# Two attentions of a one-core kernel: 64x64 tiles in the first, denominators inverted in compact form in the second

## The chip, the core and the metric

The kernel runs on one NeuronCore of a Trainium2 chip. The core has a matrix engine (TensorE, PE in the profile), a vector engine (VectorE, DVE), a scalar engine (ScalarE, ACT), a general engine (GpSimd, POOL) and a queue that only issues transfers (SyncE, SP). TensorE writes its results to PSUM, eight banks of 512 float32 a partition, which VectorE and ScalarE read. The metric is the device time of one execution, in microseconds (us). Lower is better.

## What is computed

Four layers run one after the other on 2 x 1024 tokens of 128 features, each with a normalisation before it and a residual around it: an attention of 16 heads of 64 features, a feed-forward layer with weights quantised to four bits, mixture-of-experts layers of 16 experts, and between them a second attention of 16 heads of 8 features with a bias by distance. The change touches the two attentions. The first one:

```python
def _L0_attn_ref(x, Wq, Wk, Wv, Wo):
    H, DH = (16, 64); SOFTCLAMP = 50.0; SCALE = DH ** (-0.5)
    q = jnp.einsum('bnd,fd->bnf', x, Wq).reshape(b, n, H, DH).transpose(0, 2, 1, 3)
    ...  # k and v alike, from Wk and Wv
    sim = jnp.einsum('bhid,bhjd->bhij', q, k) * SCALE
    sim = SOFTCLAMP * jnp.tanh(sim / SOFTCLAMP)
    sim = jnp.where(jnp.tril(jnp.ones((n, n), dtype=bool)), sim, jnp.finfo(sim.dtype).min)
    out = jnp.einsum('bhij,bhjd->bhid', jax.nn.softmax(sim, axis=-1), v)
    return jnp.einsum('bnf,df->bnd', out.transpose(0, 2, 1, 3).reshape(b, n, H * DH), Wo)
```

And the core of the second:

```python
    bias = slopes[:, None, None] * jnp.minimum(idx[None, :] - idx[:, None], 0)
    scores = jnp.einsum('bhtd,bhsd->bhts', q, k) / math.sqrt(D) + bias[None]
    y = jnp.einsum('bhts,bhsd->bhtd', jax.nn.softmax(scores, axis=-1), v)
    return y.transpose(0, 2, 1, 3).reshape(B, T, C) @ W_proj + b_proj
```

Both softmaxes are divided out at the end: the exponentials are multiplied with the values, and the product is scaled by the inverse of their sum.

## The kernel before

Everything is written out by hand: each engine has its own program, the engines wait for each other on counters (semaphores), and an engine does its work in the order in which it is written.

**First attention** (`stage_front`). Heads are taken in pairs, two heads side by side in 128 partitions, and each pair has two batches: 16 passes `s = 2 * p + b`, in `pair(p, more)`. The first and the last pair are written out, the six between them are a loop (`Fori`), in which waits go against a register. The lower triangle of 8 x 8 blocks of 128 x 128 is cut into NU = 9 units a pass (`PIECES`), each 512 columns wide. For a unit TensorE makes the scores of both heads (`scores`, L774: 64 rows of the array by 128 columns for each head, written 64\*128), ScalarE does tanh and exp (L486, L491), POOL masks the diagonal (L463), VectorE and POOL add up the exponentials (L403, one head each), and TensorE multiplies with the values (`multiply`, L786: 128 rows by 64 columns a head, 128\*64). `project` makes queries, keys and values of the next pass (L756, L762, also 128\*64), `totals` the sums over keys (L798, 128\*32), `out` the final product (L836). The order on TensorE goes by slots of two units: scores of the next two units, a piece of `project`, products of these two. `take` (L496, ScalarE) copies the product out of its two banks, which there are once. A float32 matmul is two instructions on the chip, so four matmuls are eight records in a profile.

**Second attention** (`stage_alibi_attention`). 16 halves `hs` of eight units `gu`, four heads together. TensorE makes scores twice: once 12 units ahead for the maxima (`max_pair`, L2112), which VectorE reduces (`reduce_chunk`, L1977, four a unit) out of a ring of three banks, and once for the exponentials (L2136, L2140); ScalarE does exp (L1911), and TensorE multiplies with values and a row of ones (L2157), so that the denominators come out beside the product. The SP queue lays each half's maxima into rows (`maxima_rows`, L1671), loads the rows of the scores of coming steps (L1686, L1727), and in `keep_out` stores a finished half to memory and loads it again in another arrangement (L1753, L1756), the denominators of four heads spread over eight features each (L1757). In `divide(k)`, for k in order 3, 0, 1, 2, VectorE inverts a quarter of them as 128 x 512 (L1994) and multiplies (L1996); three quarters after unit 117, the last after unit 124. `project_out(k)` (L2190) waits for them, on TensorE after units 119 and 126. The last half goes through `select_last` (L2167) and `divide_last` (L2002, L2005).

Of the kernel before, what the change touches and what calls it, by code (L numbers as in the profile page):

```python
# [42 lines left out]
def bcast(ap, shape):  # L43
    return ap.broadcast_to(shape)
# [133 lines left out]
class QuantFfn:  # L178
# [89 lines left out]
    def next_keep(self, act, k):  # L268
# [11 lines left out]
PIECES = [[(0, 0, 0, 512)], [(0, 0, 512, 512)],  # L280
# [4 lines left out]
NU = len(PIECES)  # L285

DIAGS = [[at for J, at, q, w in u if q == P * J] for u in PIECES]
ADDS = [[(0, 128, (0, 0), None)],
        [],
        [(512, 512, (1, 0), (2, 0))],  # L290
        [(128, 384, (0, 128), (3, 0)), (896, 128, None, (3, 384))],
        [(512, 512, None, (4, 0))],
        [(256, 256, None, (5, 0)), (768, 256, None, (5, 256))],
        [(512, 512, None, (6, 0))],
        [(384, 128, None, (7, 0)), (640, 384, None, (7, 128))],
        [(512, 512, None, (8, 0))]]
# [3 lines left out]
SLOTS = NU  # L300

# [7 lines left out]
def stage_front(nc, g, sem):  # L309
# [11 lines left out]
     z.multiplied, z.taken, z.summedA, z.summedB, z.totalled, z.copied, z.spread, z.inverted, z.kept,  # L321
     z.broad, z.scaled, z.wo, z.summed, z.added) = (
        sem("at0_" + x) for x in (
        "w ones pooled projected query key value scored clamped exped masked multiplied taken summedA summedB "
        "totalled copied spread inverted kept broad scaled wo summed added").split())
    with ExitStack() as tmp:
# [56 lines left out]

        def add_up(eng, s, b, u, h, done):
# [5 lines left out]
            for k, (to, w, first, second) in enumerate(ADDS[u]):  # L390
                into = ACC[b][:, h, to:to + w]
                if second is None:
                    if h == 1:

                        eng.sem_inc(z.pooled, 1)
                    eng.tensor_copy(into, PR[first[0]][:, h, first[1]:first[1] + w]).then_inc(done, 1)
                    continue
# [3 lines left out]
                else:  # L401
                    old = PR[first[0]][:, h, first[1]:first[1] + w]
                eng.tensor_tensor(into, old, PR[second[0]][:, h, second[1]:second[1] + w], ALU.add).then_inc(done, 1)  # L403

        with nc.Block() as block:
# [48 lines left out]
            def _(pool):  # L454
                def mask(s, u):
# [4 lines left out]
                    even = DIAGS[u] == [0, 2 * P]  # L460
                    for at in DIAGS[u][0:1] if even else DIAGS[u]:
                        blocks = v[:, at // P::2 if even else 4, :]
                        last = pool.affine_select(out=blocks, in_=blocks, compare_op=ALU.is_ge, fill=0.0, base=0,  # L463
                                                  pattern=[[0, 4 if even else 2], [1, P]], channel_multiplier=-1)
# [14 lines left out]
            def _(act):  # L479
                def clamp(s, b, u):  # L480
                    act.wait_ge(z.scored, NU * s + u + 1)
                    wait(act, z.multiplied, NU * (s - 1) + u + 1)
                    through = ADDED[max(u, 3) + 1] - ADDED[NU]
# [9 lines left out]
                def take(s, b, p, half):  # L493

                    act.wait_ge(z.multiplied, NU * s + NU - 1 + half)
# [3 lines left out]
                def pair(p, more):  # L499
                    for k in range(SLOTS):  # L500
# [4 lines left out]
                        if k == 0 and not (isinstance(p, int) and p == 0):  # L505
                            for half in range(2):
                                take(2 * p - 1, 1, p - 1, half)
                        if k in (4, 5):
                            take(2 * p, 0, p, k - 4)
# [103 lines left out]
            def _(dve):  # L613
# [11 lines left out]

                def copy_totals(s):
# [14 lines left out]
                def pair(p, more):  # L641
                    first = isinstance(p, int) and p == 0
                    for k in range(SLOTS):
                        for s, b, u in slot(p, k):
                            add_up(dve, s, b, u, 0, z.summedA)
                        if k < 3 or 4 <= k < 7 and more:
                            projected(2 * p + 1 + k // 4, 1 - k // 4, 2 * (k % 4))
                            projected(2 * p + 1 + k // 4, 1 - k // 4, 2 * (k % 4) + 1)
                        if not first:
                            if k == 0:  # L650
                                invert(2 * p - 2)
# [1761 lines left out]
```

## Time and profile before

| | us |
|---|---|
| median of 3 runs | 1230.98 |
| lowest and highest run | 1230.45, 1236.72 |
| the profiled execution, its own time | 1236.2 |
| its span, first to last instruction | 1234.5 |

A row of a timeline has the start in us, the length in us, the engine, the line of the kernel, the instruction, what it writes and reads, shape and count; idle time before it and who ended it stand in brackets. PEld are the loads of weights into the array, which run beside matmuls. A row of several instructions covers them from the first start to the last end. In the profiled execution the first attention's passes run from about 58 to 431 us, the second attention's stage from about 642 to 1070 us.

### The profile page before, as it was taken

The numbers are of one execution on the slowest core, as the hardware profiler recorded it, in microseconds if no ns is written. First come the engines' busy times: TensorE is split into PE (matmuls) and PEld (weight loads), VectorE is DVE, ScalarE is ACT, GpSimd is POOL, SyncE is SP. The second block draws the span as 40 slices with busy tenths as digits, with TensorE's granted clock in tenths as the row PEclk, the third lists the DMA queues.
The fourth block names the chain that finished last, engine by engine and source line by source line (L and its number), as shares of the span: only waits on it lengthen the run. The fifth ranks groups of instructions, "written<-read, shape, count | busy, mean of one in ns | idle before, by whom it ended". The sixth has DMA issues, their size and how long they took to land. (4 is left out here: it accounts for less than half of the span.)

```text
span 1234.5 us, 21616 instructions
## 1 busy us (share of the span) xinstructions
PE 1149.7 (93%) x7431; PEld 576.2 (47%) x7431; DVE 850.4 (69%) x1779; ACT 718.9 (58%) x944; POOL 531.2 (43%) x577
## 2 busy tenths in 40 slices
PE   4899999999999998879997999999999998787998
PEld 1444444444444485368984222222222222546896
DVE  6366667666666555864426899999999996585442
ACT  3687787787787615612215177777777776451221
POOL 0056656656756700338853014322422331035884
PEclk9899999999999998979999999999999998697999
DMA  4001001001011100427752212211121110223765
GB/s 127 1 7 25 19 24 41 18 24 38 21 24 35 30 25 6 170 65 194 178 116 63 71 42 61 65 53 54 56 60 58 55 38 14 92 84 99 194 171 122
DMA packets 56194, 81.41 MB, mean 66 GB/s; under 512 B 19348, under 2 KB 37144, under 8 KB 55472
## 3 DMA queue, kind: packets, MB, share of 16 engines
q1 hardware_dynamic: 44040, 70.30, 18.6%
q0 software_dynamic: 10880, 8.86, 4.9%
q10 hardware_dynamic: 1192, 1.19, 0.3%
q8 instruction: 48, 0.79, 0.3%
q14 instruction: 34, 0.28, 0.1%
HBM read 55.02 MB, written 15.60 MB: 57 GB/s over the span
## 5 line engine op out<-in xcount | busy, mean ns | idle before, releaser
L1911 ACT ACTIVATE at_PR<-psum 128x1024 f32<-128x1024 f32 x256 | 248.1, 1021 | 110.8 <-PE psum L2140 108.8
L1977 DVE TENSOR_REDUCE at_MX<-psum 128x1 f32<-128x512 f32 x468 | 298.7, 685 | 11.3 <-PE psum L2112 8.1
L486 ACT ACTIVATE PR<-psum 128x1024 f32<-128x1024 f32 x144 | 141.0, 1027 | 73.5 <-PE psum L774 60.2
L774 PE MATMUL psum<-Q,K 64*128 64x512 f32 (+3 forms) x768 | 143.5, 502 | 1.2 <-ACT PR L486 1.2
L491 ACT ACTIVATE PR<-PR 128x1024 f32<-128x1024 f32 x144 | 144.6, 1062 | 0.0
L786 PE MATMUL psum<-PR,V 128*64 128x512 f32 (+3 forms) x768 | 137.4, 489 | 0.1
L2157 PE MATMUL psum<-at_PR,at_VG 128*32 128x512 f32 x1024 | 136.8, 607 | 0.0
L1848 POOL TENSOR_TENSOR at_PR<-at_PR,at_FAC 128x512 f32<-128x512 f32 x64 | 81.2, 1268 | 107.1 <-ACT at_PR L1911 107.1
L463 POOL TENSOR_SCALAR_AFFINE_SELECT PR<-PR 128x256 f32<-128x256 f32 (+1 forms) x112 | 59.1, 542 | 158.0 <-ACT PR L491 157.5
L1456 PE MATMUL psum<-moe_XGT,moe_WE 128*128 128x256 f32 x512 | 124.5, 388 | 1.2 <-ACT moe_XGT L1144 1.2
L1141 ACT ACTIVATE moe_GL<-psum 128x512 f32<-128x512 f32 x64 | 38.2, 597 | 132.4 <-PE psum L1456 111.2
L2112 PEld LDWEIGHTS psum<-at_KU,at_QU 64*128 64x128 bf16 x512 | 28.2, 92 | 170.9 <-DVE at_MX L1977 143.3
L2112 PE MATMUL psum<-at_KU,at_QU 64*128 64x512 bf16 x512 | 100.1, 385 | 6.7 <-DVE at_MX L1977 1.8
L774 PEld LDWEIGHTS psum<-Q,K 64*128 64x128 f32 x768 | 64.2, 186 | 78.6 <-issue 62.8
L1456 PEld LDWEIGHTS psum<-moe_XGT,moe_WE 128*128 128x128 f32 x512 | 94.7, 195 | 12.1 <-issue 1.3
L2136 PE MATMUL psum<-at_QU,at_KU 64*128 64x512 bf16 x512 | 98.3, 379 | 0.3
L2140 PE MATMUL psum<-at_QL,at_KL 58*128 58x512 bf16 x512 | 98.3, 379 | 0.0
L1287 DVE TENSOR_TENSOR moe_H<-moe_GL,psum 128x512 f32<-128x512 f32 x64 | 44.0, 687 | 77.9 <-ACT moe_GL L1141 67.0
L1059 POOL DMA_INDIRECT moe_XG<-moe_rows_dram,moe_IDX x64 | 64.5, 1008 | 54.1 <-DVE moe_IDX L1241 32.8
L786 PEld LDWEIGHTS psum<-PR,V 128*64 128x64 f32 x768 | 50.6, 137 | 77.8 <-issue 71.4
L403 POOL TENSOR_TENSOR ACC<-ACC,PR 128x128 f32<-128x128 f32 (+3 forms) x64 | 71.8, 1121 | 5.3 <-POOL PR L463 1.0
L1821 POOL CAST at_NMB<-at_NM 128x16 bf16<-128x16 f32 x16 | 3.2, 198 | 162.6 <-DVE at_NM L1983 162.6
(256 smaller groups left out, 1798.5 us busy)
## 6 DMA issues: line engine op xcount, KB each, us to landing
moe_WE<-in_c_We SPq DMA_DIRECT2D x32, 768.0 KB
XB<-at_r_dram SPq DMA_DIRECT2D x32, 256.0 KB, 3.9
at_outs_dram<-at_OTS SPq DMA_DIRECT2D x15, 256.0 KB, 2.2
moe_rows_dram<-XNS SPq DMA_DIRECT2D x2, 1152.0 KB, 10.4
moe_spare_dram<-moe_zeros SPq DMA_DIRECT2D x2, 1024.0 KB, 13.1
moe_sum_dram<-XB SPq DMA_DIRECT2D x2, 1024.0 KB, 3.9
moe_SG<-moe_spare_dram SPq DMA_DIRECT2D x8, 256.0 KB, 4.9
at_KU<-in_c_max_krows SPq DMA_DIRECT2D x16, 128.0 KB
```

The costliest lines, as they stand in the source:

```text
L486: act.activation(PR[u][:, :, :], S[(b + u) % 2][:, :, :], ACT.Tanh, scale=SCALE0 / CLAMP).then_inc(z.clamped, 1)
L491: act.activation(PR[u][:, :, :], PR[u][:, :, :], ACT.Exp, scale=CLAMP).then_inc(z.exped, 1)
L774: mm = pe.matmul(S[(b + u) % 2][:, h, at:at + w], K[row[h], b, j * P:(j + 1) * P], Q[row[h], b, q:q + w], start=True, stop=True)
L786: mm = pe.matmul(O[row[h], q:q + w], V[:, b, j, row[h]], PR[u][:, h, at:at + w], start=(u < 2), stop=(u >= NU - 2), skip_group_check=True)
L1456: mm = pe.matmul(ps[4 + 2 * m + h][:, j * CAP:(j + 1) * CAP], WE[:, e % DEEP, at:at + P], XGT[:, e % 2, :], start=True, stop=True)
L1848: pool.tensor_tensor(pr, pr, FAC[:, 4 * (s // 2):4 * (s // 2) + 4, :], ALU.mult).then_inc(z.factored, 1)
L1911: act.activation(PR[:, gu % PRS, 2 * r:2 * r + 2, :].rearrange("p h n -> p (h n)"), g.psum[:, 2 * r * BANK:(2 * r + 2) * BANK], ACT.Exp).t ...
L1977: dve.tensor_reduce(MX[:, c // 32 % 2, 8 * (c % 2) + 4 * pair + I % 4, khalf:khalf + 1], bank(("max", c))[:, :], AX, ALU.max).then_inc(z.r ...
L2112: mm = pe.matmul(bank(("max", c + h))[:, :], queries(QU[rows, s % UPPERS, pair, :])[:, I // 4, I % 4, :], KU[rows, s % UPPERS, pair, khalf ...
L2136: pe.matmul(ps[2 * j + a].rearrange("p (i n) -> p i n", n=P), KU[rows, s % UPPERS, j, J * P:(J + 1) * P], queries(QU[rows, s % UPPERS, j, ...
L2140: mm = pe.matmul(ps[2 * j + a].rearrange("p (i n) -> p i n", n=P), KL[rows, s % LOWERS, j, J * P:(J + 1) * P], queries(QL[rows, s % LOWERS ...
L2157: mm = pe.matmul(O[32 * h:32 * h + 32, :], VG[:, s % 2, J, h, :], PR[:, gu % PRS, h, :], start=(J == 0), stop=(J == BT - 1), skip_group_ch ...
```

## The change

In the first attention all scores, products with the values and projections inside the loop become matmuls on 64 x 64 tiles of the array, four side by side. A score matmul is cut by its columns; a product and a projection are cut by their rows into two halves that accumulate, and the half that goes first (`halved`, `part_projected`) and the half that ends are separate steps. The blocks are arranged anew (`ORDER`, `BLOCKS`), so that the halves of a unit go to different banks; a unit is still 512 columns. Scores run four units ahead (`AHEAD`) and single units take the place of slots of two. `take` moves from ScalarE to VectorE.

In the second attention the denominators of a half are loaded as 128 x 16, inverted so (`invert`), stored to memory and spread over the features by a further load (`keep_inverse`). `divide` has no inversion left. The denominators of the last half are turned by TensorE, inverted as 128 x 16 and spread by TensorE (`turn_last`, `spread_last`). The quarters 3 and 0 are divided after unit 117, quarter 1 after unit 122, quarter 2 after the last unit; `project_out(1)` stands after unit 124, `project_out(2)` after the last unit.

```diff
+ORDER = [2, 3, 4, 5, 0, 1, 6, 7]
+BLOCKS = [[(0, 2), (0, 3), (0, 0), (0, 1)], [(0, 4), (0, 5), (0, 6), (0, 7)], [(1, 2), (1, 3), (1, 6), (1, 7)],
+          [(2, 2), (2, 3), (2, 6), (2, 7)], [(3, 4), (3, 5), (3, 6), (3, 7)], [(3, 3), (5, 5), (1, 1), (7, 7)],
+          [(4, 4), (4, 5), (4, 6), (4, 7)], [(1, 4), (1, 5), (5, 6), (5, 7)], [(2, 4), (2, 5), (6, 6), (6, 7)]]
...
@@ scores @@
-                            mm = pe.matmul(S[(b + u) % 2][:, h, at:at + w], K[row[h], b, j * P:(j + 1) * P],
-                                           Q[row[h], b, q:q + w], start=True, stop=True)
+                            for c in range(2):
+                                into, of = S[(b + u) % 2][row[c], h, at:at + w], Q[row[h], b, q:q + w]
...
+                                mm = pe.matmul(into, K[row[h], b, j * P + DH0 * c:j * P + DH0 * (c + 1)], of,
+                                               start=True, stop=True, skip_group_check=True)
@@ multiply @@
-                            mm = pe.matmul(O[row[h], q:q + w], V[:, b, j, row[h]], PR[u][:, h, at:at + w],
-                                           start=(u < 2), stop=(u >= NU - 2), skip_group_check=True)
-                    mm.then_inc(z.multiplied, 1)
+                    for n in range(2):
+                        for side in range(2):
+                            rows = row[side if first != swap else 1 - side]
+                            for j, at, q, w in PIECES[u][side][n:n + 1]:
+                                for h in range(2):
+                                    mm = pe.matmul(O[row[h], q:q + w], V[rows, b, j, row[h]], PR[u][rows, h, at:at + w],
...
+                    mm.then_inc(z.halved if first else z.multiplied, 1)
@@ TensorE's order @@
+                    for n in range(2 * NU if more else 2 * NU - AHEAD):
+                        turned = n == 0 or n == NU and more
+                        if turned:
...
+                            project(2 * p + 1 + n // NU, 1 - n // NU, 0, True)
+                            scores(*unit(n + AHEAD))
+                        multiply(*unit(n), n % 2 == 1, True)
+                        if turned:
+                            project(2 * p + 1 + n // NU, 1 - n // NU, 0, False)
+                        else:
+                            scores(*unit(n + AHEAD))
+                        multiply(*unit(n), n % 2 == 1, False)
+                        k = n % NU
+                        if 1 <= k <= 4 and (n < NU or more):
+                            project(2 * p + 1 + n // NU, 1 - n // NU, (k + 1) // 2, k % 2 == 1)
+                        if n == 5 and not begin:
                             totals(2 * p - 1, 1, 4 * p + 4)
@@ VectorE, first attention @@
+                        if n == 1 and not first:
+                            take(2 * p - 1, 1, p - 1)
+                        if n == 10:
+                            take(2 * p, 0, p)
@@ second attention, SP @@
-                    sp.dma_start(DEN[rows, columns], bcast(outs_dram[hs, :, DH1:DH1 + 1, :], [4, DH1, BANK])).then_inc(z.loads[k], 16)
+                    sp.dma_start(DR[:, hs % 2, :], outs_dram[hs, :, DH1:DH1 + 1, :].rearrange("h o (p k) -> h (o p) k", k=16)
+                                 ).then_inc(z.dens, 16)
+                def keep_inverse(hs):
+                    q, k = hs // 4, hs % 4
+                    sp.wait_ge(z.inverted, hs + 1)
+                    sp.dma_start(inverse_dram[hs].rearrange("h o (p k) -> h (o p) k", k=16), DR[:, hs % 2, :]).then_inc(z.rstored, 16)
+                    sp.wait_ge(z.rstored, 16 * (hs + 1))
+                    sp.dma_start(DEN[32 * q:32 * q + 32, k * BANK:(k + 1) * BANK], bcast(inverse_dram[hs], [4, DH1, BANK])
+                                 ).then_inc(z.loads[k], 16)
@@ second attention, VectorE @@
+                def invert(hs):
+                    dve.wait_ge(z.dens, 16 * (hs + 1))
+                    dve.reciprocal(DR[:, hs % 2, :], DR[:, hs % 2, :]).then_inc(z.inverted, 1)
                 def divide(k):
                     rows, columns = (P if k < 3 else P - 32), slice(k * BANK, (k + 1) * BANK)
                     dve.wait_ge(z.loads[k], 128 if k < 3 else 96)
-                    dve.reciprocal(DEN[0:rows, columns], DEN[0:rows, columns]).then_inc(z.inverted, 1)
-                    dve.wait_ge(z.inverted, DIVIDED.index(k) + 1)
                     dve.tensor_tensor(g.XT[0:rows, columns], g.XT[0:rows, columns], DEN[0:rows, columns], ALU.mult).then_inc(z.yt, 1)
+                    if gu % BT == 6 and gu > BT:
+                        invert(gu // BT - 1)
                     if gu == FIRST_OUT:
-                        for k in DIVIDED[:3]:
-                            divide(k)
+                        divide(3)
+                        divide(0)
...
+                    elif gu == SECOND_OUT:
+                        divide(1)
...
+                invert_last()
+                divide(2)
+                norm_apply_vector(dve, g, last_norm, 0, g.XNS)
+                divide_last()
+                add_out(2)
```

On TensorE, at the start of the loop of the first attention, stood this (Q, K, V and PR are the operands of scores and products, XT and Wqkv those of projections; 128x512 is the size of the output; REGISTER_ALU and ISA rows are the register work of the waits):

```order
L774 MATMUL psum<-Q,K 128x512 x2
L306 REGISTER_ALU
L774 MATMUL psum<-Q,K 128x384 x2
L774 MATMUL psum<-Q,K 128x128 x2
L306 REGISTER_ALU
L306 ISA
L756 MATMUL psum<-XT,Wqkv 64x512 x4
L780 ISA
L306 REGISTER_ALU
L380 ISA
L786 MATMUL psum<-PR,V 64x512 x4
```

Now the same place reads:

```order
L803 ISA
L814 MATMUL psum<-XT,Wqkv 64x512 x4
L321 ISA
L841 MATMUL psum<-Q,K 64x512 x4
L848 ISA
L396 ISA
L860 MATMUL psum<-PR,V 64x256 x4
L807 ISA
L814 MATMUL psum<-XT,Wqkv 64x512 x4
L853 REGISTER_ALU
L860 MATMUL psum<-PR,V 64x256 x4
```

Scores that wrote 128 partitions write 64, one unit of scores and half a product stand where two units stood, and a projection has a first and a last part around them. Within the loop body there are 376 matmuls where there were 152, and 49 other instructions where there were 43.

On VectorE, around one half of the second attention (MX and NM are the maxima, MR their rows, DR the compact denominators), the order is now:

```order
+L2100 CAST at_MR<-psum 32x128
+L2089 TENSOR_REDUCE at_MX<-psum 128x1 x8
+L2105 RECIPROCAL at_DR<-at_DR 128x16
+L2089 TENSOR_REDUCE at_MX<-psum 128x1 x20
+L2095 TENSOR_REDUCE at_NM<-at_MX 128x16
```

The reciprocal stands among the 28 reduces that followed the cast before. On the SP queue one half read as follows (KU and QL are operands of coming scores, OTS the finished half, DEN the spread denominators):

```order
L1686 DMA at_KU<-at_SPL 8x2x1024 x4
L1753 DMA at_outs_dram<-at_OTS 128x512
L1756 DMA XT<-at_outs_dram 32x1x512
L1757 DMA at_DEN<-at_outs_dram 32x1x512
L1671 DMA at_QL<-at_MR 1x8x128 x4
```

And now, with `keep_inverse` ahead of `keep_out`:

```order
+L1781 DMA at_KU<-at_SPL 8x2x1024 x4
+L1859 DMA at_inverse_dram<-at_DR 128x16
+L1861 DMA at_DEN<-at_inverse_dram 32x1x512
+L1848 DMA at_outs_dram<-at_OTS 128x512
+L1851 DMA XT<-at_outs_dram 32x1x512
+L1852 DMA at_DR<-at_outs_dram 128x1x16
+L1766 DMA at_QL<-at_MR 1x8x128 x4
```

The store and the load of the inverses stand ahead of the next half's `keep_out` and of its maxima rows; before, the three transfers of `keep_out` followed the loads directly.

## Rows read from the trace of the kernel before

**Rows 1.** The page: each engine's busy time, its share of the span, instructions.

```profile
PE 1149.7 (93%) x7431; PEld 576.2 (47%) x7431; DVE 850.4 (69%) x1779; ACT 718.9 (58%) x944; POOL 531.2 (43%) x577
```

**Rows 2.** Stretches: span; busy (x) of PE, PEld, DVE, ACT, POOL; clock; DMA.

```profile
245.54:292.00 46.46, 46.46 (x306) 20.01 (x304) 30.97 (x40) 36.46 (x41) 30.03 (x37) 1.00 0.10 28
...
700.00:1000.00 300.00, 293.10 (x2222) 80.91 (x2220) 288.15 (x473) 220.14 (x234) 86.67 (x114) 1.00 0.19 56
```

**Rows 3.** Timeline, TensorE, slots and a total of the first attention.

```profile
206.47 1.94 PE L756 MATMUL psum<-XT,Wqkv 128*64 128x512 f32 x8
208.24 1.89 PE L786 MATMUL psum<-PR,V 128*64 128x512 f32 x12
210.06 2.00 PE L774 MATMUL psum<-Q,K 64*128 64x512 f32 x12
211.99 1.97 PE L762 MATMUL psum<-Wqkv,XT 128*64 128x128 f32 x32
213.79 1.89 PE L786 MATMUL psum<-PR,V 128*64 128x512 f32 x12
...
217.53 1.06 PE L798 MATMUL psum<-ACC,ones 128*32 128x512 f32 x8
218.52 1.94 PE L786 MATMUL psum<-PR,V 128*64 128x512 f32 x12
```

**Rows 4.** Timeline, weight loads inside a product of the first attention.

```profile
208.24 0.14 PEld L786 LDWEIGHTS psum<-PR,V 128*64 128x64 f32 x2 [0.29 <-issue]
208.67 0.14 PEld L786 LDWEIGHTS psum<-PR,V 128*64 128x64 f32 x2 [0.29 <-issue]
```

**Rows 5.** Timeline, eight short matmuls after a wait; and one such load alone.

```profile
534.96 0.29 PEld L1434 LDWEIGHTS psum<-moe_LS,spread 64*128 64x128 f16 x8 [0.78 <-DVE moe_LS L1236]
...
L1434 PEld LDWEIGHTS psum<-moe_LS,spread x64: 92/101/115, 535.0 to 1130.3; 64*128 64x128 f16 x64
```

**Rows 6.** The page, a DMA queue of instructions: packets, MB, share.

```profile
q8 instruction: 48, 0.79, 0.3%
```

**Rows 7.** ACT and DVE around the change of passes, first attention.

```profile
200.38 1.08 ACT L496 ACTIVATE OT<-psum 128x512 f32 x2
...
203.56 0.24 DVE L633 RECIPROCAL RC<-RC 128x16 f32<-128x16 f32 x1
...
213.38 1.31 DVE L623 COPY V<-psum 128x512 f32<-128x512 f32 x2
```

**Rows 8.** Timeline, VectorE, one half of the second attention.

```profile
978.01 18.09 DVE L1977 TENSOR_REDUCE at_MX<-psum 128x1 f32<-128x512 f32 x28 [0.39 <-PE psum L2112]
```

**Rows 9.** Timeline, SP queue, keep_out and maxima_rows of one half.

```profile
948.86 0.44 SPq L1753 DMA_DIRECT2D at_outs_dram<-at_OTS  x1
953.17 0.65 SPq L1756 DMA_DIRECT2D XT<-at_outs_dram  x1
953.87 0.63 SPq L1757 DMA_DIRECT2D at_DEN<-at_outs_dram  x1
956.30 3.04 SPq L1671 DMA_DIRECT2D at_QL<-at_MR  x4
```

**Rows 10.** Waits of the SP queue (us, times, longest); issues with us to landing.

```profile
SPq L1671 <- DVE at_MR L1988: 56.0, 15, 11.9
...
at_r_dram<-RC SPq DMA_DIRECT2D x16, 8.0 KB, 1.5
```

**Rows 11.** Timeline, TensorE and ACT after unit 119 of the second attention.

```profile
1024.33 1.94 ACT L1911 ACTIVATE at_PR<-psum 128x1024 f32<-128x1024 f32 x2 [0.27 <-PE psum L2140]
...
1030.90 2.08 PE L2190 MATMUL psum<-WP,XT 128*128 128x128 f32 x8 [2.77 <-DVE XT L1996]
...
1033.99 1.94 ACT L1911 ACTIVATE at_PR<-psum 128x1024 f32<-128x1024 f32 x2 [7.72 <-PE psum L2140]
```

**Rows 12.** Timeline, VectorE after the last unit: the last half's inversion and division.

```profile
1053.94 3.36 DVE L2002 RECIPROCAL at_DEN<-psum 32x512 f32<-32x512 f32 x1 [1.13 <-PE psum L2167]
1057.34 0.70 DVE L2005 TENSOR_TENSOR XT<-psum,at_DEN 32x512 f32<-32x512 f32 x1
```

More of the change, by code:

```diff
@@ L300 @@
 SLOTS = NU
+AHEAD = 4
 def wait(eng, sem, value):
@@ L389, in add_up @@
                 unit_done(eng, s, u)
-            for k, (to, w, first, second) in enumerate(ADDS[u]):
-                into = ACC[b][:, h, to:to + w]
+            for k, (n, to, first, second) in enumerate(ADDS[u]):
+                into = split(ACC[b][:, h, :], n)[:, to, :]
                 if second is None:
@@ L395, in add_up @@
                         eng.sem_inc(z.pooled, 1)
-                    eng.tensor_copy(into, PR[first[0]][:, h, first[1]:first[1] + w]).then_inc(done, 1)
+                    eng.tensor_copy(into, split(PR[first[0]][:, h, :], n)[:, first[1], :]).then_inc(done, 1)
                     continue
@@ L401, in add_up @@
                 else:
-                    old = PR[first[0]][:, h, first[1]:first[1] + w]
-                eng.tensor_tensor(into, old, PR[second[0]][:, h, second[1]:second[1] + w], ALU.add).then_inc(done, 1)
+                    old = split(PR[first[0]][:, h, :], n)[:, first[1], :]
+                eng.tensor_tensor(into, old, split(PR[second[0]][:, h, :], n)[:, second[1], :], ALU.add).then_inc(done, 1)
         with nc.Block() as block:
@@ L504, in pair @@
                             exponent(s, u)
[L505 to L509, printed above, removed]
                 def first_copies(first, end):
@@ L624, in projected, with take @@
                                         ).then_inc(z.value, 1)
+                def take(s, b, p):
+                    dve.wait_ge(z.multiplied, NU * s + NU)
+                    for half in range(2):
+                        dve.tensor_copy(heads_out(p, b, half * BANK, (half + 1) * BANK), O[:, half * BANK:(half + 1) * BANK]
+                                        ).then_inc(z.taken, 1)
                 def copy_totals(s):
@@ L802, in pair @@
                 def pair(p, more):
[L803 to L824 removed]
+                    begin = isinstance(p, int) and p == 0
@@ new lines, in pair @@
+                    if not more:
+                        pe.wait_ge(z.wo, 16)
+                        for n in (14, 15, 16):
+                            multiply(*unit(n), False, True)
+                        totals(2 * p, 0, 4 * p + 4)
+                        pe.wait_ge(z.clamped, 2 * NU * PAIRS)
+                        out(0, 0, 1)
+                        pe.wait_ge(z.halved, NU * last + NU - 1)
+                        for n in (14, 15, 16):
+                            multiply(*unit(n), False, False)
+                        multiply(*unit(17), True, True)
+                        out(0, 1, 2)
+                        multiply(*unit(17), True, False)
@@ L881, in _ @@
                 for k in (4, 5):
-                    project(0, 0, k)
-                scores(0, 0, 0)
-                scores(0, 0, 1)
-                pe.wait_ge(f1.next.xt, 4)
+                    project_first(k)
+                for u in range(AHEAD):
+                    scores(0, 0, u)
+                    if u == 1:
+                        pe.wait_ge(f1.next.xt, 4)
                 span(pair)(pe)
@@ L1777, in _ @@
                     if s == STEPS1:
+                        keep_inverse(hs - 2)
                         continue
```

275 lines of the change are left out of this document (165 added, 110 removed), and 4 rows, old and new, of the table PIECES.

## The prediction, made before the changed kernel ran

> **What bounds the kernel now.** I read the page first: TensorE is busy for 93% of the span, no other engine over 69% [rows 1]. That is a mean over stages, so next came the stretches. A pair of passes of the first attention takes 46.46 us, all of it TensorE's, at the full granted clock; ACT has 36.46, VectorE 30.97, POOL 30.03 [rows 2]. There only TensorE counts. In 300 us of the second attention's loop VectorE is busy 288.15, and TensorE's 293.10 is for the most part matmuls that are queued [rows 2]: the timeline shows VectorE's 28 reduces back to back in 18.09 us, 0.646 each, with 0.39 idle ahead of them [rows 8]. There VectorE sets the pace. Then came the timelines of TensorE at the places of the change [rows 3, 4, 11], the queues [rows 9, 10] and the page's list of DMA queues [rows 6].
>
> **First attention: what the gaps are worth.** Inside a product one matmul of 512 columns (two loads, two matmul records) follows the other after 0.43 us [rows 4]; a group of four is 1.71 at full rate. A pair has 24 such groups (nine slots of scores and products, six projections) and two totals of half the length: 24 x 1.706 + 2 x 0.853 = 42.65. The pair takes 46.46, so 3.8 are lost. The starts in the timeline say where. Scores to projection: 1.93; projection to product, both on 128\*64: 1.77; product to scores: 1.82; totals to product: 0.99 instead of 0.85 [rows 3]. Against 1.71 that is 0.22 where 64\*128 ends, 0.11 where it begins and 0.06 where the shape stays: 0.39 a slot. With all on 64\*64 the shape changes at the two totals alone, and I leave 0.38 for each total: 42.65 + 0.75 = 43.4, 3.05 less than now. That counts for 7.5 of the 8 pairs. In the last pass no projection stands, and ACT's 1.9 a unit ((36.46 - 2 x 1.08) / 18 by [rows 2, 7]) is as long as TensorE's half slot. 7.5 x 3.05 = **-22.9**. That four tiles work side by side is shown by the totals, whose eight records of 512 columns take 1.06 [rows 3]. The others fit into 43.4: VectorE with 31.0 + 2.7, ACT with 36.5 - 2.2.
>
> - Scores four units ahead at the very start wait for the clamp of an earlier unit: half of ACT's 1.9, **+0.9** (0 to 1.9).
> - `take` on VectorE: two copies of 512 took 1.31 there, 1.08 on ACT [rows 7]. While it runs, TensorE has half a projection and one unit of scores to do, 1.71. The copies with a handover at each end (0.27, as ACT's after TensorE in [rows 11]) are 1.85. 0.15 x 16 passes = **+2.4**; 0 if nothing shows, 4.8 if VectorE is in the middle of an addition.
>
> First attention: -19.6.
>
> **Second attention.** Each half gets a compact reciprocal on VectorE. One of 128x16 took 0.24 in the first attention [rows 7]; I take 0.22 as its part of the pace. 13 of the 15 lie where VectorE is the bound: **+2.9** (2.3 to 3.1).
>
> What goes is the three large inversions after unit 119. ACT's exp ends at 1026.3 and the next begins 7.72 later; `project_out` stood on TensorE until VectorE had divided (2.77), and its eight matmuls then took 2.08 [rows 11]. From one exp to the next are 9.66 us. With the divisions of 0.70 [rows 12] done early and one `project_out` left (four matmuls of 128 columns, 0.85 at the rate of [rows 4]), I expect 1.94 + 0.85 + a handover of 0.27 = 3.1: **-6.6**. Next in line there is the exp itself, so no more can come.
>
> At the end the inversion of 3.36 [rows 12] becomes one of 128x16 with two turns through TensorE: 0.2 + 0.3 of VectorE and 2.0 to 2.6 for the matmuls and handovers. This alone would be about -0.6. But divide, `project_out` and addition of quarter 2 (0.7, 1, 0.7 with statistics behind them) come down into the tail and partly stand in line with it: **+0.8** net (-0.6 to +2).
>
> The SP queue: `keep_inverse` puts a store (issue about 0.4, landing 1.5, as the 8 KB of [rows 10]) and a spreading load (issue 0.63 to 0.65 [rows 9]) ahead of `keep_out` and of the maxima rows, 2.2 to 2.6 us a half. Behind it stand the stores of the finished half, and TensorE, which scores from those rows. SP waits for VectorE's cast before them 56.0 / 15 = 3.7 us on average [rows 10], which covers it. But in the half shown `keep_out`'s wait took from 948.86 to 953.17 and the rows started at 956.30, 1.8 us after the issue before them ended [rows 9]. There it comes up to 0.8 late in one half of three, 5 halves of 15, and TensorE's queue absorbs some 0.4 of it: **+1** (0 to 6, all 15 late by 0.4).
>
> Second attention: 2.9 - 6.6 + 0.8 + 1 = -1.9. **Sum: -21.5.** The profiled execution took 1236.2 by its own time; changed, it would be 1214.7. It lies near the slowest of the three runs, 5.2 over the median, so I carry the difference over: 1231.0 - 21.5 = 1209.5, **1210**.
>
> **Rival 1, slower: TensorE's instructions don't come fast enough.** A pass has 305 records (306 + 304 in a pair by [rows 2]) and will have 752. Most new groups hold 32 in 0.853 us, 27 ns each. But the two halves of the V projection (64 each), the scores of the diagonal unit (64) and its two half products (32 each) are 256 records in 3.41 us: 13.3 ns each. For it: eight loads with eight matmuls of eight columns, which give the array nearly nothing to do, took 0.29, with 0.10 for the last load: 0.19 / 7 = 27 ns a pair, 13.6 a record [rows 5]. That is at the limit, costs 16 x 256 x 0.0003 = 1.2 us and lies in the range. Against more: nothing in the trace is slower than that under full supply. The price at x ns is 16 x (256x - 3413): it decides from 19 ns on, where the 22.9 are eaten; at 20 it gives 1237, at 28 (the spacing of the V projection now, 64 records in 1.80 [rows 3], where the array is the bound) 1270. Chance 0.16.
>
> The Trainium skill, "TensorE: Matmul & The Clock Gate", section "Wait — 56ns, not 53.3ns?", says that with hardware decoding off each MATMUL costs the sequencer about 62 ns, and with it on starts come no closer than about 25 ns. By the first the change would lose over 70 us, as an estimate from that page; by the second it would lose nothing. The 27 ns a pair that this trace shows speak for the second.
>
> **Rival 2: the loop no longer stays in the instruction memory.** TensorE's loop body grows from 152 x 4 + 43 = 651 instructions to 376 x 4 + 49 = 1553. The instruction queue moved 48 packets, 0.79 MB, 16 KB each [rows 6]; TensorE's program with the body counted once is 2 x 7431 records [rows 1] less five repeats of 608, and some 400 others: 12,200 instructions, 48 packets of 256. So the 651 stayed. If 1553 don't, the five jumps back wait for a fetch: 1.5 us at least (the smallest landing, [rows 10]), three times that at most, +7.5 to +22, that is 1217 to 1231; one and a half in the middle, 1225. Chance 0.13. The Trainium skill, "Runtime: NRT & Kernel Launch", section "Instruction fetch mechanics", gives PE's memory as 2048 instructions and says that a taken branch out of the fetched window stalls. By the first number the new body still fits; no row here shows it.
>
> **Rival 3: the gaps don't come from the tile's shape,** but go with each new group of weights. Then the first attention gains nothing and pays for `take`: 1229 to 1231. Against it: the step between two groups of equal shape, 1.77, is the smallest of the three [rows 3]. Chance 0.06.
>
> **How the numbers follow.** The forecast has 0.62; its own range is 1203 (`take`, start and SP at nothing and the tail at its lower end: -5.7) to 1219 (`take`, SP, start and tail at their upper ends: +9.6). Rival 1 has 0.16, rival 2 0.13, rival 3 0.06, and 0.03 is left for others. The range goes to 1240: it takes in rivals 2 and 3 and rival 1 up to 20 ns, and leaves out about 0.12. About 0.5%, 6 us, is what a measurement can tell from no change. Faster: 0.62 and 0.10 of rival 2 = 0.72. Same: 0.03 of rival 2, rival 3 and 0.02 of others = 0.11. Slower: rival 1 and 0.01 = 0.17.
>
> **What the changed profile would show.** A pair of 43.4 in the stretches, with ACT and VectorE below 36; if it is over 46, the timeline tells rival 1 (dense groups longer than 0.853 with loads at equal spacing) from rival 3 (every group longer). The instruction queue with some 60 packets; with rival 2 over 80 and a gap of TensorE at each third pair's start, where the jump is. At the passes' change `take` right behind the product and TensorE's wait of 0.1 to 0.3 for it. In the second attention, per half, 0.2 more of VectorE; SP's idle time ahead of the maxima rows down by 2.2 to 2.6; no inversion of 512 and no gap of 7.7 on ACT; SP late would show as TensorE waiting for the maxima rows and VectorE behind it. I am wrong if 64\*64 tiles don't run four wide with float32, if the dense groups take over 19 ns a record, or if ACT turns out to follow TensorE's order of products so closely that it becomes the bound at 43.4.

## The result: 0.992 of the time before, under half of what was forecast

| | us |
|---|---|
| before, median of 6 runs | 1230.92 |
| changed, median of 6 runs | 1222.41 |
| lowest and highest run of the changed kernel | 1220.35, 1226.75 |
| ratio, with its 95% interval | 0.9922 (0.9902 to 0.9942) |
| the same comparison on another chip (e9) | 0.9943 (0.9924 to 0.9962) |
| changed, the profiled execution's own time and span | 1226.15, 1224.4 |

The change gains 7.0 to 9.6 us by the two ratios, not 21.5. The time lies outside the forecast's own range of 1203 to 1219; that it lies in the stated one is luck, since that was widened for rivals which did not happen. The sum was wrong: the first attention gained a sixth of its term, and the second more than its own.

The stretches of the profile of the changed kernel; columns are the span, the busy time (x instructions) of PE, PEld, DVE, ACT and POOL, the clock, the DMA share and GB/s. The first is a pair of passes, the second lies in the second attention:

```profile
239.71:285.44 45.73, 44.26 (x752) 27.45 (x753) 33.88 (x43) 34.48 (x36) 29.23 (x31) 1.00 0.11 28
700.00:1000.00 300.00, 292.35 (x2234) 80.08 (x2232) 288.93 (x486) 222.53 (x236) 87.87 (x115) 1.00 0.20 56
```

A pair takes 45.73 instead of 46.46 [rows 2]; 43.7 was forecast with `take`. TensorE is idle for 1.47 us of it, for the first time. The timeline of TensorE over part of a pair says where (a row's start, length, engine, line, instruction, and in brackets the idle time with who ended it):

```profile
268.16 1.04 PE L814 MATMUL psum<-XT,Wqkv 64*64 64x512 f32 x8
269.02 1.04 PE L841 MATMUL psum<-Q,K 64*64 64x512 f32 x8
270.18 0.66 PE L860 MATMUL psum<-PR,V 64*64 64x256 f32 x8
...
280.13 1.07 PE L841 MATMUL psum<-Q,K 64*64 64x256 f32 x16
281.00 0.64 PE L860 MATMUL psum<-PR,V 64*64 64x256 f32 x8
281.43 1.08 PE L818 MATMUL psum<-Wqkv,XT 64*64 64x128 f32 x32
282.30 0.64 PE L860 MATMUL psum<-PR,V 64*64 64x128 f32 x16
282.74 1.06 PE L841 MATMUL psum<-Q,K 64*64 64x512 f32 x8
283.60 0.64 PE L860 MATMUL psum<-PR,V 64*64 64x128 f32 x16
285.44 1.06 PE L873 MATMUL psum<-XN,ones 128*32 128x512 f32 x8 [1.20 <-DVE V L643]
286.44 0.66 PE L860 MATMUL psum<-PR,V 64*64 64x256 f32 x8
```

- The groups themselves do what was forecast: the step from one to the next is 0.86 or 0.87 where their columns need 0.853, whatever the two groups are. What [rows 3] showed at the changes of shape is gone.
- The dense group of the V projection (32 matmul records with as many loads, 281.43) takes 0.87 as well: 13.6 ns a record. Instructions come fast enough.
- At the change of passes the products start 1.16 after scores that need 0.86: 0.3 us of waiting for `take`, twice a pair. VectorE's two copies end at 269.83 there, 0.35 before the products start at 270.18.
- Ahead of the totals of every second pass TensorE waits. The products before end 0.43 after 283.60, at 284.03, and the totals start at 285.44: **1.4 us**, a pair, of which the change of shape alone would take 0.14 (totals of the first pass, 261.95, start 0.57 after products of 0.43). What it waits for are VectorE's copies of V, since projection and totals write the same bank. The forecast had no such wait. Over the whole first attention it is 8.2 us in 7 waits (us, times, longest):

```profile
PE psum L873 <- DVE V L643: 8.2, 7, 1.2
```

VectorE in the same stretch:

```profile
278.54 2.00 DVE L666 TENSOR_TENSOR OT<-OT,XB 128x1024 f32 x1
280.46 0.62 DVE L429 TENSOR_TENSOR ACC<-PR 128x256 f32<-128x256 f32 x1
281.12 3.07 DVE L429 TENSOR_TENSOR ACC<-ACC,PR 128x256 f32<-128x256 f32 x2
284.11 1.27 DVE L643 COPY V<-psum 128x512 f32<-128x512 f32 x2
```

V was projected by 282.3, and the copies start at 284.11, behind two additions of 1.38 and 1.66 us. The first was nearly done when V was ready, the second ran from 282.53 on. The order of VectorE's program put them there.

The page's DMA queue of instructions, where [rows 6] had 48 packets; 59 is what the larger program needs once (2 x 10981 records less five repeats of 1504, and some 400 others, by 256: 58), so the loop body of 1553 instructions is not fetched again, and no gap stands at the loop's start:

```profile
q8 instruction: 59, 0.97, 0.3%
```

In the second attention a half of the loop (from one cast to the next) takes 21.35 us before and now. VectorE in one half:

```profile
738.72 0.27 DVE L2100 CAST at_MR<-psum 32x128 bf16<-32x128 f32 x1
739.38 5.14 DVE L2089 TENSOR_REDUCE at_MX<-psum 128x1 f32<-128x512 f32 x8 [0.39 <-PE psum L2239]
744.44 0.24 DVE L2105 RECIPROCAL at_DR<-at_DR 128x16 f32<-128x16 f32 x1
744.60 12.87 DVE L2089 TENSOR_REDUCE at_MX<-psum 128x1 f32<-128x512 f32 x20
```

8 reduces, the reciprocal and 20 reduces take 739.38 to 757.47, 18.09 us. Before, the 28 reduces alone took 18.09 [rows 8]. The reciprocal costs nothing. The rows at unit 119, where [rows 11] had idle times of 7.72 on ACT and 2.77 on TensorE:

```profile
1021.86 1.94 ACT L2020 ACTIVATE at_PR<-psum 128x1024 f32<-128x1024 f32 x2 [0.82 <-PE psum L2267]
1023.18 1.16 PE L2328 MATMUL psum<-WP,XT 128*128 128x128 f32 x8
1024.92 1.94 ACT L2020 ACTIVATE at_PR<-psum 128x1024 f32<-128x1024 f32 x2 [1.12 <-PE psum L2267]
```

From exp to exp across `project_out` it is 3.06 us, to the tenth what was forecast, instead of 9.66.

Stage by stage, from the starts of rows in the two profiled executions (first scores; first transposes of the feed-forward layer; first reduce of the second attention; its last cast; first instruction of the experts):

| stretch | before | changed | difference |
|---|---|---|---|
| first attention, scores to last output | 57.36 to 457.94, 400.6 | 59.23 to 456.38, 397.2 | -3.4 |
| second attention, first reduce to last cast | 673.69 to 1018.61, 344.9 | 670.82 to 1015.59, 344.8 | -0.1 |
| last cast to the experts | 1018.61 to 1071.15, 52.5 | 1015.59 to 1062.66, 47.1 | -5.5 |

That is -9.0; what is left of the spans' difference of 10.1 lies in the stages that nothing changed. The other profiles say how far such a difference can be trusted. The first attention of the changed kernel is 396.7 long in e1 and in e9, 0.5 less than here. The stretch from the last cast to the experts is 51.8 in e1, which has it as before, and 46.9 in e9 and 45.5 in e2, which have it changed: -4.7 to -7.1.

### The profile page after: what moved, and what is told of

It reads as the page before. It is cut to its first block and busy times, and to the rows that moved or that the text cites. A ratio compares the mean times of both kernels' runs of the same rounds, so it can differ in the third digit from the quotient of the medians.

```text
span 1224.4 us, 29054 instructions
## 1 busy us (share of the span) xinstructions
PE 1129.5 (92%) x10981; PEld 631.5 (52%) x10981; DVE 856.5 (70%) x1805; ACT 704.5 (58%) x915; POOL 522.8 (43%) x529
## 5 line engine op out<-in xcount | busy, mean ns | idle before, releaser
L511 ACT ACTIVATE PR<-psum 128x1024 f32<-128x1024 f32 x144 | 145.7, 1022 | 83.1 <-PE psum L841 74.7
L860 PE MATMUL psum<-PR,V 64*64 64x256 f32 (+1 forms) x2560 | 171.7, 357 | 5.1 <-issue 1.5
L841 PE MATMUL psum<-Q,K 64*64 64x512 f32 (+2 forms) x1792 | 151.5, 437 | 2.1 <-ACT PR L511 2.1
L860 PEld LDWEIGHTS psum<-PR,V 64*64 64x64 f32 x2560 | 96.9, 133 | 102.3 <-issue 90.4
L841 PEld LDWEIGHTS psum<-Q,K 64*64 64x64 f32 x1792 | 68.2, 133 | 26.3 <-issue 10.5
L1159 POOL TENSOR_TENSOR moe_SG<-moe_SG,XN 128x512 f32<-128x512 f32 x16 | 20.3, 1270 | 123.7 <-ACT XN L1202 108.2
```

Source lines behind the costliest of these rows:

```text
L511: act.activation(PR[u][:, :, :], S[(b + u) % 2][:, :, :], ACT.Tanh, scale=SCALE0 / CLAMP).then_inc(z.clamped, 1)
L841: mm = pe.matmul(into, K[row[h], b, j * P + DH0 * c:j * P + DH0 * (c + 1)], of, start=True, stop=True, skip_group_check=True)
L860: mm = pe.matmul(O[row[h], q:q + w], V[rows, b, j, row[h]], PR[u][rows, h, at:at + w], start=(first and u == 0), stop=(not first and u == ...
```

## Experiments

**e1 and e2: each part alone.** The two halves of the diff touch different functions.

```diff
  e1: stage_front of the changed kernel, stage_alibi_attention of before
  e2: stage_front of before, stage_alibi_attention of the changed kernel
```

> The first attention's change alone, the second attention as before. The changed kernel's profile has a pair of passes at 45.73 us where 43.4 was forecast and 46.46 stood before, and the whole first attention shorter by about 3.4. Theory 1 (the first attention gained little, the second what was forecast): about -4, 1227, with pairs at 45.7. Theory 2 (the two parts disturb each other or the profiled execution's split is accidental): clearly off that, -8 or more or no gain at all. Both: pairs of 45.7.

> The second attention's change alone, the first attention as before. Theory 1: the parts add up, so this one brings -5 to -6, 1225: the loop's half stays at 21.35 us although it holds a reciprocal more, ACT's idle time of 7.7 after unit 119 falls to about 0.3 to 1.5, and from the last reduce of the loop to the experts' first instruction it is 5.5 shorter. Theory 2: it brings less than 3, since the shorter time in the changed kernel came from elsewhere.

e1: 0.9971 (0.9950 to 0.9993), about -3.6 us. e2: 0.9962 (0.9937 to 0.9987), about -4.7. Theory 1 holds for both, e2 a little under its 5 to 6: they add up to -8.3, and each agrees with its line of the table (-3.4, -5.5) within its interval. A pair is 45.73 in e1; a half of the loop is 21.35 in e2 too, and ACT's idle time across `project_out` 1.12. So the two parts can be judged apart, and what is missing is missing in the first attention.

**e3: `take` back on ScalarE.** Is it that VectorE has two copies a pass more to do?

```diff
@@ ScalarE, order of a pair @@
                         for s, b, u in slot(p, k):
                             clamp(s, b, u)
+                            if k == 6 and u == 3:
+                                for half in range(2):
+                                    take(2 * p, 0, p, half)
+                        if k == 1 and not (isinstance(p, int) and p == 0):
+                            for half in range(2):
+                                take(2 * p - 1, 1, p - 1, half)
                         for s, b, u in slot(p, k):
                             exponent(s, u)
@@ VectorE @@
-                        if n == 1 and not first:
-                            take(2 * p - 1, 1, p - 1)
-                        if n == 10:
-                            take(2 * p, 0, p)
```

> The changed kernel with take on ScalarE again, between the tanh and the exp of the units that follow the change of passes. Theory A (VectorE's queue is what costs: two more copies a pass make the copies of V late, and TensorE waits for them before the totals): the 1.4 us gap ahead of the totals of every second pass goes, pairs of 44.0 to 44.4, about -9 to -11 against the changed kernel. Theory B (the handover of take at the change of passes costs, wherever it runs): only the 0.3 at each change moves, pairs of 45.1 to 45.8. Theory C (groups on 64x64 tiles are slower than their columns): nothing moves, 45.7.

1.0071 (1.0049 to 1.0094), slower than before. A pair takes 47.52 (242.75 to 290.27), which none of the theories had. TensorE at two places of it:

```profile
275.01 0.66 PE L862 MATMUL psum<-PR,V 64*64 64x256 f32 x8 [1.35 <-ACT OT L521]
...
290.27 1.07 PE L875 MATMUL psum<-XN,ones 128*32 128x512 f32 x8 [1.20 <-DVE V L649]
```

VectorE's busy time in the pair fell from 33.88 to 31.31, and the wait ahead of the totals is the same 1.20. So theory A in the form "VectorE has too much to do" is wrong. Nor did theory B hold, by which the handover costs the same wherever it runs: at one change of passes the wait grew to 1.35, since on ScalarE the rest of an exp and a tanh stand ahead of `take` when the products end (they end by 271.95, `take` starts at 273.58). At the places tried here `take` is better off on VectorE.

**e4: the copies of V ahead of an addition.** Same work, other order, at n = 5 and n = 14, which are unit 5 of the first and of the second pass:

```diff
@@ VectorE @@
                     for n in range(2 * NU):
+                        if n == 5:
+                            projected(2 * p + 1, 1, n - 1)
+                            projected(2 * p + 1, 1, n)
+                        if n == 14 and more:
+                            projected(2 * p + 2, 0, n - 10)
+                            projected(2 * p + 2, 0, n - 9)
                         add_up(dve, 2 * p + n // NU, n // NU, n % NU, 0, z.summedA)
-                        if n in (1, 3, 5):
+                        if n in (1, 3):
                             projected(2 * p + 1, 1, n - 1)
                             projected(2 * p + 1, 1, n)
-                        if n in (10, 12, 14) and more:
+                        if n in (10, 12) and more:
```

> The changed kernel with the two copies of V ahead of the additions of units 5 and 14 on VectorE, which wait for ACT's exp and POOL's mask, instead of behind them. Nothing else moves; take stays on VectorE. Theory A in its form that the order counts, not the load: the gap of 1.4 ahead of the totals goes, pairs of 44.3 to 44.6, -8 to -10 against the changed kernel. If the load counts: a new wait as large comes elsewhere (ACT's tanh waits for the additions), pairs stay over 45.3. Theory C: 45.7.

0.9878 (0.9849 to 0.9907), about -15 against before where the changed kernel had -7 to -10; the 5 to 8 between them are less than the 8 to 10 expected. The same two places on VectorE and TensorE:

```profile
276.32 1.39 DVE L429 TENSOR_TENSOR ACC<-ACC,PR 128x256 f32<-128x256 f32 x1
277.74 1.29 DVE L643 COPY V<-psum 128x512 f32<-128x512 f32 x2
```

```profile
277.51 0.64 PE L866 MATMUL psum<-PR,V 64*64 64x128 f32 x16
277.95 1.06 PE L847 MATMUL psum<-Q,K 64*64 64x512 f32 x8
278.81 0.64 PE L866 MATMUL psum<-PR,V 64*64 64x128 f32 x16
279.38 1.07 PE L879 MATMUL psum<-XN,ones 128*32 128x512 f32 x8
```

The copies start 0.2 after V's projection, and the totals 0.57 after the products of 0.43: the bare change of shape. The pair is 44.46 (234.92 to 279.38), 1.27 less, in the expected span, and no new wait came up. The waits for V are gone from the whole first attention, which is 388.9 long, 8.3 less. VectorE is busy for 34.49 of the pair, more than the 33.88 of the changed kernel. So the order is the cause, and not the load. The addition that now stands behind the copies takes 0.68 there instead of 1.66; only its length in the old place made the order cost so much.

**e7: more work in front of the products that wait for `take`.** On top of e4:

```diff
@@ TensorE @@
                             project(2 * p + 1 + n // NU, 1 - n // NU, 0, True)
                             scores(*unit(n + AHEAD))
+                            project(2 * p + 1 + n // NU, 1 - n // NU, 0, False)
                         multiply(*unit(n), n % 2 == 1, True)
                         if turned:
-                            project(2 * p + 1 + n // NU, 1 - n // NU, 0, False)
+                            scores(*unit(n + AHEAD + 1))
+                        elif k == 1 and projects:
+                            project(2 * p + 1 + n // NU, 1 - n // NU, 1, True)
                         else:
                             scores(*unit(n + AHEAD))
```

> The kernel with V's copies first (e4), and on TensorE at the change of passes the second part of the projection and the next unit's scores moved: half projection, scores, half projection, then the products that wait for take. The cover of take grows from 1.71 to 2.57 us of work, where its two copies and handovers need 2.0. Theory A: the gap of 0.3 at each change of passes goes, a pair of 43.8 to 43.9 instead of 44.46, -4 to -5 against e4, some -19 against before. Rival: scores that go a unit earlier wait for ACT's tanh, and the gap moves there; pairs of 44.4 or more.

0.9816 (0.9794 to 0.9837), 1213.14 beside 1236.19 of before on that chip, 23 us where some 19 were expected. A pair:

```profile
236.19:279.92 43.73, 43.73 (x756) 25.55 (x752) 33.38 (x42) 34.47 (x37) 29.27 (x30) 1.00 0.12 29
```

43.73, and TensorE is never idle. With this the first attention is 383.3 long (56.26 to 439.55), 17.3 less than before and 5.6 less than in e4.

**e8: the last pass too.** On top of e7, in the pass without projections:

```diff
@@ TensorE @@
+                        if n == NU and not more:
+                            scores(*unit(n + AHEAD))
                         multiply(*unit(n), n % 2 == 1, True)
                         if turned:
                             scores(*unit(n + AHEAD + 1))
                         elif k == 1 and projects:
                             project(2 * p + 1 + n // NU, 1 - n // NU, 1, True)
-                        else:
+                        elif n < NU or more:
                             scores(*unit(n + AHEAD))
+                        elif n + AHEAD + 1 < 2 * NU:
+                            scores(*unit(n + AHEAD + 1))
```

> e7 with one thing more: in the last pass, which has no projections, unit 4's scores stand ahead of the first products that wait for take, and scores run five units ahead from there on. In e7 TensorE waits 1.66 us there and 1.06 for POOL's mask near the end. Theory A (take is uncovered there, for the first products follow the last ones directly): the wait falls by 0.86 to about 0.8, -0.9 against e7, up to -2 if ACT then is ahead of the mask. Rival (the last pass is bound by ACT, as the forecast said): the wait moves to the mask or to the last products and nothing is gained, within 0.5 of e7. Against before about -23 to -24.

> The changed kernel once more, beside e8 on the same chip: some -9.6 against before as in the comparison, so that the gap between it and the version of the experiments is read on one chip: 12 to 14 us. If the runs on this chip gave it -15 or more, the gain of e4 and e7 would be smaller than it looks.

TensorE at the change to the last pass, in e7 and then in e8:

```profile
390.91 0.66 PE L866 MATMUL psum<-PR,V 64*64 64x256 f32 x8 [1.47 <-issue]
...
400.84 1.79 PE L866 MATMUL psum<-PR,V 64*64 64x128 f32 x32 [1.06 <-POOL PR L488]
```

```profile
392.23 0.66 PE L866 MATMUL psum<-PR,V 64*64 64x256 f32 x8 [0.61 <-issue]
...
401.84 0.66 PE L866 MATMUL psum<-PR,V 64*64 64x256 f32 x8 [0.26 <-ACT PR L516]
```

The wait for `take` falls by 0.86 and the one for POOL's mask is gone but for 0.26 of waiting for ACT. The first attention is 381.8 long (57.66 to 439.42), 1.5 less than in e7, theory A. The rival has its share all the same: in the part of the last pass that is left, ACT never stops (columns as above).

```profile
391.48:402.73 11.25, 10.28 (x192) 6.48 (x192) 7.33 (x9) 11.25 (x13) 9.49 (x10) 1.00 0.19 50
```

As a whole e8 has 0.9822 (0.9794 to 0.9850), 22 us where 23 to 24 were expected: 1209.92 beside 1231.30 of before and 1225.05 of the changed kernel (e9) on the same chip. The gap to the changed kernel is 15 us, where e9 expected 12 to 14, since the changed kernel gained less here (-7.0) than in its first comparison. The runs can't tell e7 from e8 (other chips, overlapping intervals); their profiles can. Both beat both kernels, e7 the changed one by 13 to 16 us by its ratio.

**e5: is VectorE the bound of the second attention's loop?** Four more reciprocals a half.

```diff
                     dve.wait_ge(z.dens, 16 * (hs + 1))
+                    for n in range(4):
+                        dve.reciprocal(RE[:, 2 * n:2 * n + 2, :].rearrange("p h d -> p (h d)"), DR[:, hs % 2, :])
```

> The changed kernel with four more reciprocals of 128x16 ahead of the one of each half in the second attention, written to a place that nothing reads then. A half of the loop took 21.35 us both without a reciprocal and with one. Theory 1 (VectorE sets the pace, and the one reciprocal fell into small waits for TensorE that the timeline hides inside a row of reduces): four more, 0.16 us each from start to start, are past that slack; a half becomes 21.9 to 22.1, the kernel +7 to +10. Theory 2 (TensorE's own order sets the pace and VectorE follows it): a half stays at 21.35 to 21.45, the kernel within 2 us of the changed one.

```profile
739.63 0.27 DVE L2100 CAST at_MR<-psum 32x128 bf16<-32x128 f32 x1
740.29 5.15 DVE L2089 TENSOR_REDUCE at_MX<-psum 128x1 f32<-128x512 f32 x8 [0.39 <-PE psum L2241]
745.35 0.58 DVE L2106 RECIPROCAL at_RE<-at_DR 128x16 f32<-128x16 f32 x4
745.84 0.20 DVE L2107 RECIPROCAL at_DR<-at_DR 128x16 f32<-128x16 f32 x1
745.96 12.85 DVE L2089 TENSOR_REDUCE at_MX<-psum 128x1 f32<-128x512 f32 x20
...
761.41 0.27 DVE L2100 CAST at_MR<-psum 32x128 bf16<-32x128 f32 x1
```

A half takes 21.78 (739.63 to 761.41), 0.43 more, for five reciprocals that occupy 0.61 from the first's start to the next reduce. So theory 1 in kind, a little under its size: VectorE sets the pace, with a slack of about 0.18 a half (0.61 less 0.43) in waits that the timeline doesn't show, and one reciprocal of 0.16 just fits into it. The kernel ran once, 1233.4, and the changed one did not run on that chip, so this rests on the profile alone.

**e6: is it the change of shape?** The kernel before, with the scores alone on 64x64 tiles.

```diff
-                            mm = pe.matmul(S[(b + u) % 2][:, h, at:at + w], K[row[h], b, j * P:(j + 1) * P],
-                                           Q[row[h], b, q:q + w], start=True, stop=True)
+                            for c in range(2):
+                                mm = pe.matmul(S[(b + u) % 2][row[c], h, at:at + w], K[row[h], b, j * P + DH0 * c:j * P + DH0 * (c + 1)],
+                                               Q[row[h], b, q:q + w], start=True, stop=True, skip_group_check=True)
```

> The kernel before with the scores of the first attention alone on 64x64 tiles, products and projections still on 128x64. Theory 1 (what is lost is the change of tile shape between groups, whatever the two shapes are): each slot still has its two changes, a pair stays at 46.2 to 46.8. Theory 2 (groups of 64x128 are the slow ones, since they go two side by side across all columns): the 0.22 a slot behind the scores goes, 18 groups, a pair of 44 to 44.6.

```profile
246.14 1.95 PE L777 MATMUL psum<-Q,K 64*64 64x512 f32 x24
248.02 1.94 PE L756 MATMUL psum<-XT,Wqkv 128*64 128x512 f32 x8
249.79 1.89 PE L789 MATMUL psum<-PR,V 128*64 128x512 f32 x8
251.61 1.95 PE L777 MATMUL psum<-Q,K 64*64 64x512 f32 x24
```

Scores to projection 1.88, projection to product 1.77, product to scores 1.82: the steps of [rows 3], with 0.05 off the first. The pair is 46.12 (246.14 to 292.26), just below the span of theory 1 and far from theory 2; the kernel's one run took 1236.09, beside 1236.19 of before. What costs is that two groups differ in shape, and 64\*64 for the scores alone gets little of it back; the same shape throughout does, as the steps of 0.86 show.

## Why the prediction was wrong, step by step

- **Value of one shape throughout** (42.65 of columns and 0.38 for each total, 43.4 a pair): right. e7 gives 43.73 with nothing waiting; the totals cost 0.31 each there beyond their columns, and the rest is 0.007 for each of the pair's 66 groups. e8's first attention is 18.8 shorter than before, where the forecast had 19.6.
- **"The others fit into 43.4: VectorE with 31.0 + 2.7"**: this step failed. The busy time was right (33.88), but it is no proof that an engine is in time. The slack of 10 us a pair says nothing of one copy behind two additions, on which a bank and so TensorE's next group depend. It cost 1.27 us a pair and 8.2 in all, half of the 16.2 that the first attention's term is off by: e4 takes back 5 to 8 by its ratio and 8.3 by its profile (397.2 to 388.9 for the first attention). The place could be seen ahead: `projected` behind `add_up` at n = 14, and between the end of V's projection and the totals TensorE has 1.7 us of work (282.30 to 284.03) where it had 3.7 (213.79 to 217.53 [rows 3]). I had counted VectorE's time there and not its order.
- **`take`** at +0.15 a pass: this size was wrong as well. It is 0.3 in the trace (0.37 by the 0.73 that e7 takes off e4's pair), and 1.66 in the last pass, where no projection covers it and the forecast had counted nothing for it. Together 6 to 7 us against 2.4; e7 and e8 take off 5.6 and 1.5. The forecast had 0.27 from the end of the copies to the products; it is 0.35 in the loop and 0.10 in the last pass, which is written out, and what makes this difference no run shows.
- **Start with four units ahead, +0.9**: TensorE waits 0.82 more for ACT before the first product. Right.
- **Last pass bound by ACT**, with no gain there: right so far, but it was lengthened. From the totals before it to its own it took 26.61 before (403.50 to 430.11), 28.68 changed (399.87 to 428.55) and 27.23 in e8 (384.37 to 411.60). In e8, behind what is left of the wait for `take`, ACT is busy throughout (11.25 of 11.25).
- **+2.9 for the reciprocals**: 0. The bound was named rightly (e5), but 0.39 us of idle time in a half is only what the timeline prints; short waits between back-to-back rows hold 0.18 more. My lower bound should have been zero.
- **-6.6 at unit 119 and +0.8 in the tail**: -5.8 against -5.5 measured from the last cast on (-4.7 to -7.1 with the other profiles). Right.
- **SP queue, +1**: TensorE waits twice for the maxima rows, 0.8 us together; VectorE then waits 0.49 in one half and 0.26 in another. Right in kind, and in size as far as these waits go; in the stretch's sum (-0.1) it can't be told from zero.
- **Rival 1** (feeding): out, dense groups take 0.87. **Rival 2** (instruction memory): out, 59 packets. **Rival 3** (no gain from the shape): out by e6 and e7. The kind of rival that was missing is the one that happened: a copy late by its place in another engine's program.

## What to carry to other kernels

When the bounding engine gets faster, read the order of every engine that hands it a buffer, copy by copy, with the work that stands ahead of each; busy shares don't answer it. Operations that free a bank go ahead of those that only have to be done sometime. And where an operation is added to an engine that seems to have no idle time left, zero belongs into its range: e5 found 0.18 us a half that no row shows. All three are advice drawn from this kernel alone.

## What the runs showed of the hardware

Between groups of float32 matmuls TensorE loses 0.22 us where a 64\*128 group ends and a 128\*64 one begins, and 0.11 on the way back; between two 128\*64 groups it is 0.06, which is no change of shape. That makes the 0.39 a slot of [rows 3]. With 64x64 throughout the step is the columns' time and 0.01. The Trainium skill, "TensorEngine Tiling (Array Packing)", section "Key Properties", says that changing the tiling mode drains TensorE; the rows agree that a change costs time, e6 with two other shapes too (0.17 and 0.11), and give it its price here.

Additions of one line on VectorE took very different times, all those in the changed kernel as minimum/median/maximum in ns:

```profile
L429 DVE TENSOR_TENSOR XN<-XN,PR x48: 508/692/1587, 71.3 to 402.6; 128x512 f32<-128x512 f32 x40, 128x256 f32<-128x256 f32 x8
L429 DVE TENSOR_TENSOR ACC<-ACC,PR x48: 510/1103/1749, 92.4 to 422.1; 128x512 f32<-128x512 f32 x40, 128x256 f32<-128x256 f32 x8
```

The long ones go with additions of POOL, and they are what the copies of V waited for: of this line's 144 additions on VectorE 51 took over 1.1 us, each with an addition of POOL beside it for at least half of its time, and of the 31 with next to none beside them none took over 1.03. The Trainium skill, "GPSIMD Engine Reference", section "8. Key points", says that GpSimd shares its SBUF interfaces with VectorE, with contention where VectorE reads two SBUF inputs. That fits, but no run here took POOL's additions away, so the cause is argued and not shown, and so is why the second pass of a pair has more of them.
